# From the scan to the feed-forward: the last chunk computes no state, its row norm moves to the vector engine, and the first gate weights are split in two halves

## The chip, the core and the metric

The kernel runs on one core of a Trainium2 chip. The metric is the device time of one launch in microseconds; lower is better. Engines are named as the profile names them: PE (matrix products and transposes), PEld (its weight loads), DVE, ACT, POOL, and SP, which here only starts transfers.

## The reference

The input `x` has 2048 rows of 512. Each row is normalised, goes through one mixer layer, and then through a mixture of experts:

```python
x = x + attn(layernorm(x))          # attn: the layer below
x = x + experts(layernorm(x))       # 8 experts of width 352, 2 for each row

def attn(x0):
    h = rmsnorm(x0, ln1_w)
    h = x0 + mamba2(h)              # projection, conv, chunked scan, gated norm, out_proj
    h2 = rmsnorm(h, ln2_w)
    return h + silu(h2 @ gate_w) * (h2 @ up_w) @ down_w      # 512 -> 2048 -> 512
# in mamba2, the rows are 16 chunks of 128, with one state per head carried on:
#   states_c = B^T (decay * xdt);  carry_{c+1} = states_c + decay_c * carry_c
#   y_c = Y_diag_c + C_c carry_c ;  out = rmsnorm(y * silu(z), norm_w) @ out_proj_w
```

The state that the last chunk leaves is used by nobody.

## The kernel before, in words

Four stages follow one another, each a block in which every engine has its own list of instructions; all engines meet at the end of a block. `project` makes the products of `in_proj_w` and the convolution; `ssd` is the chunked scan; `feed_forward` is the dense gated layer; `experts` routes the rows and runs the experts. The change lies at the end of `ssd` and the start of `feed_forward`.

**The scan.** The order of the work is written out by hand. A loop runs c = 0 to 17 on every engine. In step c, chunk c is computed (`now`, c < 16), the out projection and row norms of chunk e = c-1 are finished (`late`), and the normed rows of chunk f = c-2 are turned and put into the feed-forward's input (`later`). So step 16 has only e = 15 and f = 14, and step 17 only f = 15. In step 16:

- PE: `out_proj(15, 0)` (12 matmuls L1132), `row_sums(15)` (L1140), `turn_h2(14)` (4 transposes L1154), `out_proj(15, 1)` (12 matmuls). In step 15 it ends with `states(15)` (8 matmuls L1110).
- DVE: `gate(15, 1)`, `low(15, 1)` (L929), `new_carry(15)` (L979), `squares(15)` (L936), `row_sums(15)` (a copy, L941), `h2_low(14)` (L952), `outcome(15)` (L961), which writes the row result `hres`.
- ACT: `high(15, 1)`, `h2_high(14)` (L861), `h_squares(15)` (L874), which sums the squares of `hres`.
- POOL: `row_scale(15)` (L793 to L795), `residual(15)` (L803, `x0 = hres + x0`, which SP then stores as `xh` rows), `second_norm(15)`: two steps on one column (L809, L810), then two on whole rows (L811 `h2 = hres * v`, L812 `h2 = h2 * ln2_row`).

Step 17 is `turn_h2(15)` on PE, `h2_high(15)` on ACT, `h2_low(15)` on DVE. `turn_h2` and `states(15)` contain the same `wait_ge(s["h2_lo"], ...)` several times over.

**The feed-forward.** Its weights come in 8 blocks of 256 of the 2048 columns, and each block has three pieces (gate, up, down; 512 KB each). Each fp32 piece is split into a high and a low part: ACT writes `w_hi` (L1304 for block 0, L1325 later), POOL writes `w_lo = stage - w_hi` (L1278). PE multiplies high by high, high by low and low by high (L1372). A block is run over 4 steps of 512 rows: `width` (two column groups of 128, gate and up, 48 matmuls) and `out` (24 matmuls), with `width` of the next step issued ahead of `out` of this one. ACT takes the silu of a gate product (L1312), DVE multiplies it with the up product (L1338), ACT and DVE split the result (L1315, L1341). In `body(0, 1)` ACT's list has the high part of block 1's gate piece ahead of the silu of step 2:

```python
if k % NR and not (isinstance(b, int) and b == NB - 1):
    j = k % NR - 1
    eng.wait_ge(w_dma[j], b * 16 + 32)
    ...
    eng.activation(w_hi[(k // NR + 1) % 2][j][:, :], stage[j][:, :], ACT.Copy)
following(width, b, k)
```

SP's list in this block: the down piece of block 0 (L1249), the load of all `xh` rows into `acc` (4 MB, L1254), a 10 MB fill of `sorted` with `blank` (L1257), then the pieces of block 1 (L1246, L1249), all on one queue in this order. The gate and up pieces of block 0 are loaded already in step 15 of the scan.

Of the kernel before, what the change touches and what calls it, by code (L numbers as in the profile page):

```python
# [653 lines left out]
def ssd(nc, ins, dr, ident, ones, keep, ffT, first_weights, over):  # L654
# [6 lines left out]
    with ExitStack() as ctx:  # L661
# [94 lines left out]
        def _(eng):  # L756
# [48 lines left out]
            def second_norm(e):  # L805

                t, v = h2[e % 2], small[:, 5:6]
                eng.wait_ge(s["hsq"], e + 1)
                steps = [lambda: eng.tensor_scalar(v, small[:, 4:5], 1.0 / D, EPS, ALU.mult, ALU.add),  # L809
                         lambda: eng.tensor_tensor(v, v, half_neg[:, :], ALU.pow),  # L810
                         lambda: eng.tensor_scalar(t[:, :], hres[:, :], v, None, ALU.mult),  # L811
                         lambda: eng.tensor_tensor(t[:, :], t[:, :], ln2_row[:, :], ALU.mult)]  # L812
                for i, step in enumerate(steps):
                    if i:
                        eng.wait_ge(s["h2_step"], e * NH2 + i)
                    if i == 2:
                        ge(eng, s["h2T"], e - 1)
                    step().then_inc(s["h2_step"], 1)

            eng.wait_ge(s["v_dma"], 16 * 9)  # L820
            for c in range(TILES + 1):
                e = c - 1
                if c < TILES:
                    for a in range(2):
                        skip_x(c, a)
                    decayed_x(c)
                    decay_carry(c)
                if e >= 0:
                    row_scale(e)
                    residual(e)  # L830
                    second_norm(e)

        @block.scalar
        def _(eng):
# [42 lines left out]
            for c in range(TILES + 2):  # L877
                e, f = c - 1, c - 2
                now, late, later = c < TILES, 0 <= e < TILES, 0 <= f
                if now:  # L880
                    exps(c, 0)
                    cum_exp(c, 0)
                    exps(c, 1)
                if late:
                    high(e, 1)
                if now:
                    exps(c, 2)
                if later:
                    h2_high(f)
                if now:  # L890
                    exps(c, 3)
                    cum_exp(c, 1)
                    high(c, 0)
                    if c + 1 < TILES:
                        rows(c + 1)
                if late:
                    h_squares(e)
                if c == 0:
                    eng.wait_ge(s["v_dma"], 16 * 9)
                    eng.wait_ge(s["wo_dma"], 16 * 4)  # L900
                    for n in range(NB):
                        eng.activation(wo_hi[:, n, :], wo_raw[:, n, :], ACT.Copy, scale=normw[:, n:n + 1])\
                           .then_inc(s["wo_hi"], 1)

        @block.vector
        def _(eng):
# [48 lines left out]
            def outcome(e):  # L955
# [5 lines left out]
                eng.scalar_tensor_tensor(hres[:, :], o_ps[:, :], small[:, 3:4], yres[:, :], ALU.mult, ALU.add)\  # L961
                   .then_inc(s["h"], 1)

            def scaled_x(c):
                g, u = group(c)
                eng.wait_ge(s["xb_row"], c + 1)
                ge(eng, s["yd"], 2 * (c - 1))
                ge(eng, s["xdd"], c - 1)
                eng.tensor_tensor(xdt[c % 2][:, :].rearrange("p (g r d) -> p g r d", g=NG, r=HPG),
                                  xb_row[c % 2][:, 0, :].rearrange("p (g d) -> p g d", g=NG).unsqueeze(2)  # L970
                                  .broadcast_to([P, NG, HPG, HD]),
                                  dt_all[:, g, u * HEADS:(u + 1) * HEADS].rearrange("p (g r) -> p g r", g=NG).unsqueeze(3)
                                  .broadcast_to([P, NG, HPG, HD]), ALU.mult).then_inc(s["xdt"], 1)
# [16 lines left out]
            for c in range(TILES + 2):  # L990
# [7 lines left out]
                    score(c, 1)  # L998
                if late:
                    low(e, 1)  # L1000
                    new_carry(e)
                    squares(e)
                if now:
                    gate(c, 0)
                if late:
                    row_sums(e)
                if later:
                    h2_low(f)
                if now:
                    score(c, 2)  # L1010
# [2 lines left out]
                    low(c, 0)  # L1013
                if late:
                    outcome(e)
                if now:
                    if c + 1 < TILES:
                        scaled_x(c + 1)
                    rows_normed(c)
# [7 lines left out]
        def _(eng):  # L1027
# [61 lines left out]
            def states(c):  # L1089

                eng.wait_ge(s["xdd"], c + 1)
                eng.wait_ge(s["xb_row"], min(c + 2, TILES))
                if c == TILES - 1:
                    eng.wait_ge(s["h2_lo"], c - 1)
                if c == TILES - 1:
                    eng.wait_ge(s["h2_lo"], c - 1)
                if c == TILES - 1:
                    eng.wait_ge(s["h2_lo"], c - 1)
                if c == TILES - 1:
                    eng.wait_ge(s["h2_lo"], c - 1)  # L1100
                if c == TILES - 1:
                    eng.wait_ge(s["h2_lo"], c - 1)
                if c == TILES - 1:
                    eng.wait_ge(s["h2_lo"], c - 1)
                if c == TILES - 1:
                    eng.wait_ge(s["h2_lo"], c - 1)
                n = HPG * HD
                for hg in range(NG):
                    a, b = hg // 2, hg % 2
# [10 lines left out]
                    last = eng.transpose(b_ps[:, n * P:(n + 1) * P], cv[c % 2][:, n, :], ident[:, :])  # L1120
                last.then_inc(s["turn"], 1)

            def out_proj(e, a):

                if e == 0 and a == 0:
                    eng.wait_ge(s["wo_lo"], NB)
                if a == 0:
                    ge(eng, s["h"], e)
                eng.wait_ge(s["lo"], 2 * e + a + 1)
                for j in range(HPG):  # L1130
                    for t, (x, w) in enumerate(((y_hi, wo_hi), (y_hi, wo_lo), (y_lo, wo_hi))):
                        mm = eng.matmul(o_ps[:, :], x[a][:, j, :], w[:, a * HPG + j, :],  # L1132
                                        start=(a == 0 and j == 0 and t == 0), stop=(a == 1 and j == HPG - 1 and t == 2))
                mm.then_inc(s["out"], 1)
# [7 lines left out]
            def turn_h2(f):  # L1142

                eng.wait_ge(s["h2_step"], f * NH2 + NH2)
                ge(eng, s["carry"], min(f + 2, TILES))
                ge(eng, s["h2_lo"], f)
                ge(eng, s["h2_lo"], f)
                ge(eng, s["h2_lo"], f)
                ge(eng, s["h2_lo"], f)
                ge(eng, s["h2_lo"], f)  # L1150
                ge(eng, s["h2_lo"], f)
                ge(eng, s["h2_lo"], f)
                for k in range(KD):
                    last = eng.transpose(b_ps[:, k * P:(k + 1) * P], h2[f % 2][:, k * P:(k + 1) * P], ident[:, :])  # L1154
# [3 lines left out]
            for c in range(TILES + 2):  # L1158
# [9 lines left out]
                if now:  # L1168
                    diagonal(c, 0)
                    seg(c, 2)  # L1170
                    carried(c, 0)
                if late:
                    row_sums(e)
                if later:
                    turn_h2(f)
                if now:
                    b_dot_c(c, 1)
                    seg(c, 3)
                    cum_rows(c, 1)
                if late:  # L1180
                    out_proj(e, 1)
                if now:
                    if c + 1 < TILES:
                        rows(c + 1)
                    diagonal(c, 1)
                    carried(c, 1)
                    states(c)


def constants(nc, ident, ones):  # L1190
# [11 lines left out]
def feed_forward(nc, ins, dr, ffT, acc, mv, first_weights, over):  # L1202
# [7 lines left out]
    with ExitStack() as ctx:  # L1210
        def sb(name, shape, dt=F32):
# [14 lines left out]
        assert NI * D == KD * FB and TPR == 4  # L1226
        s = {n: ctx.enter_context(nc.semaphore("ff_" + n)) for n in (
            "blanked", "cleared", "acc_dma", "w_hi", "w_lo",
            "gate_ps", "up_ps", "silu", "prod", "p_hi", "p_lo", "down", "add",
            "bn", "stat")}  # L1230
        CR = 2 * TPR
        w_dma = [over["w_dma0"], over["w_dma1"], over["w_dma2"]]
        block = ctx.enter_context(nc.Block())

        def as_in(t):
            return t[:, :].rearrange("p (k n) -> p k n", k=KD)
# [5 lines left out]
        def _(eng):  # L1242
# [6 lines left out]
                    eng.dma_start(as_down(stage[j]), src).then_inc(w_dma[j], 16)  # L1249

            load_piece(0, 2)
            for i in range(3):
                eng.wait_ge(over[f"xh_st{i}"], 16 * len(range(i, TILES, 3)))
            eng.dma_start(acc[:, :, :], dr["xh"].rearrange("(t p) n -> p t n", p=P)).then_inc(s["acc_dma"], 16)  # L1254
# [12 lines left out]
        def _(eng):  # L1267
# [5 lines left out]

            def low_parts(b, par):
                for j in range(3):
                    eng.wait_ge(w_dma[j], (b + 1) * 16)
                    eng.wait_ge(s["w_hi"], b * 3 + j + 1)
                    eng.tensor_tensor(w_lo[par][j][:, :], stage[j][:, :], w_hi[par][j][:, :].bitcast(F32),  # L1278
                                      ALU.subtract).then_inc(s["w_lo"], 1)

            with eng.Fori(0, NB // 2) as i:
                for par in range(2):
                    low_parts(i * 2 + par, par)

# [16 lines left out]
        def _(eng):  # L1301
            for r in range(3):
                eng.wait_ge(w_dma[r], 16)
                eng.activation(w_hi[0][r][:, :], stage[r][:, :], ACT.Copy).then_inc(s["w_hi"], 1)  # L1304

            def width(b, k):
                step = b * NR + k % NR
# [24 lines left out]
        def _(eng):  # L1332
            def width(b, k):
                for c in range(NI):
# [6 lines left out]
                    eng.tensor_tensor(p_lo[k % 2][:, c, :], prod[c][:, :], p_hi[k % 2][:, c, :].bitcast(F32),  # L1341
                                      ALU.subtract).then_inc(s["p_lo"], 1)

            width(0, 0)
            eng.wait_ge(s["acc_dma"], 16)

# [21 lines left out]
        def _(eng):  # L1368
# [6 lines left out]
            def width(b, k):  # L1375
                par, r = k // NR % 2, k % NR
                cols = slice(r * RG, (r + 1) * RG)
                for c in range(NI):
                    n = (b * NR + r) * NI + c
                    for j, ps, free, done in ((0, gate_ps[c], "silu", "gate_ps"), (1, up_ps[c], "prod", "up_ps")):  # L1380
                        eng.wait_ge(s[free], n + 1)
                        if r == 0 and c == 0:
                            eng.wait_ge(s["w_lo"], b * 3 + j + 1)
                        for q in range(KD):
                            w = [as_in(t[par][j])[:, q, c * P:(c + 1) * P] for t in (w_hi, w_lo)]
                            x = [t[:, q, cols] for t in (hT_hi, hT_lo)]
                            mm = three(ps[:, :], w, x, q == 0, q == KD - 1)
# [537 lines left out]
```

## Time and profile before

| | us |
|---|---|
| median of 3 runs (lowest, highest) | 1609.52 (1608.76, 1609.54) |
| the profiled execution, its whole time | 1608.9 |
| its span, first to last instruction | 1607.2 |
| PE busy over the span | 1432.8 (89%) |
| DVE, ACT, POOL busy over the span | 776.9, 446.9, 441.4 |

The span is the time between the first and the last recorded instruction; 1.7 us of the execution lie around it. Times inside the trace count from the span's start. The scan ends and the feed-forward begins at 598.7 us.

### The profile page before, as it was taken

What the parts mean: (1) busy time and instruction counts of PE and PEld (TensorE: products, weight loads), DVE (VectorE), ACT (ScalarE), POOL (GpSimd) and SP (SyncE); (2) the same over time, 40 slices, a digit from 0 to 9 for tenths busy, and PEclk for the clock granted to TensorE, in tenths of its full rate; (3) what the DMA queues carried; (4) which work ended last, traced back from release to release, by engine and by line L of the source; (5) the groups of instructions that cost most, each with busy time, mean ns of one, the idle gap of its engine ahead of it and who ended that gap; (6) DMA issues with size and microseconds to landing.
All of it is one profiled execution on the core that took longest, in us unless ns stands there. A gap on an engine that the chain in (4) does not pass through costs nothing. (4 is left out here: it accounts for less than half of the span.)

```text
span 1607.2 us, 20104 instructions
## 1 busy us (share of the span) xinstructions
PE 1432.8 (89%) x6651; PEld 1035.5 (64%) x6652; DVE 776.9 (48%) x1357; ACT 446.9 (28%) x924; POOL 441.4 (27%) x486
## 2 busy tenths in 40 slices
PE   5799999799999969999999999999720899999996
PEld 4677778466666648888888888888410555555553
DVE  5868778699999852433333333334544122121211
ACT  3444444545555531222111221111210111111110
POOL 1412111277777661110101101010116122222222
PEclk9899999899999989999999999999865899999998
DMA  8123125432233229100100001000595222222220
GB/s 185 53 78 120 66 79 164 158 130 95 99 113 111 93 63 369 67 27 14 39 13 26 26 13 39 0 1 0 190 369 188 73 74 89 81 87 90 80 86 15
DMA packets 92867, 147.12 MB, mean 92 GB/s; under 512 B 29182, under 2 KB 45566, under 8 KB 92800
## 3 DMA queue, kind: packets, MB, share of 16 engines
q1 hardware_dynamic: 79424, 119.92, 22.7%
q0 software_dynamic: 8800, 25.21, 4.6%
q10 hardware_dynamic: 4576, 1.13, 0.3%
q8 instruction: 37, 0.61, 0.2%
q14 instruction: 30, 0.25, 0.1%
HBM read 91.63 MB, written 58.27 MB: 93 GB/s over the span
## 5 line engine op out<-in xcount | busy, mean ns | idle before, releaser
L1372 PE MATMUL ff_bank<-ff_hT_hi,ff_w_hi 128*128 128x512 f32 x512 | 202.2, 395 | 5.3 <-POOL ff_w_lo L1278 5.3
L1372 PE MATMUL ff_bank<-ff_hT_hi,ff_w_lo 128*128 128x512 f32 x512 | 204.4, 399 | 0.0
L1372 PE MATMUL ff_bank<-ff_hT_lo,ff_w_hi 128*128 128x512 f32 x512 | 202.6, 396 | 0.0
L1814 PE MATMUL ex_bank<-w_gu,xT 128*128 x624 | 192.8, 462 | 1.4 <-ACT xT L1745 0.8
L1338 DVE TENSOR_TENSOR ff_prod<-ff_prod,ff_bank 128x512 f32<-128x512 f32 x64 | 44.1, 688 | 267.2 <-PE ff_bank L1372 253.3
L1278 POOL TENSOR_TENSOR ff_w_lo<-ff_stage,ff_w_hi 128x1024 fp32r<-128x1024 f32 x24 | 57.5, 2400 | 408.2 <-ACT ff_w_hi L1325 408.1
L1814 PEld LDWEIGHTS ex_bank<-w_gu,xT 128*128 128x128 f32 x624 | 116.3, 191 | 60.6 <-issue 3.3
L1784 DVE SCALAR_TENSOR_TENSOR result_rows<-ex_bank,xs,result_rows 128x512 f32<-128x512 f32 x39 | 29.3, 751 | 255.9 <-DMA result_rows<-out_dram,xs 253.3
L599 PE MATMUL pj_bank<-hT_hi,w_in_hi 128*128 128x512 f32 x336 | 137.4, 409 | 10.6 <-DVE zst L525 4.6
L507 DVE SCALAR_TENSOR_TENSOR conv_acc<-raw,conv_w,conv_acc 128x512 f32<-128x512 f32 x144 | 113.9, 791 | 47.0 <-ACT raw L326 37.0
L599 PE MATMUL pj_bank<-hT_lo,w_in_hi 128*128 128x512 f32 x336 | 135.7, 404 | 0.0
L599 PE MATMUL pj_bank<-hT_hi,w_in_lo 128*128 128x512 f32 x336 | 134.3, 400 | 0.0
L1832 PE MATMUL ex_bank<-w_dn,moe_hT 128*128 (+1 forms) x234 | 111.5, 613 | 17.5 <-DVE moe_hT L1779 17.5
L1372 PEld LDWEIGHTS ff_bank<-ff_hT_hi,ff_w_hi 128*128 128x128 f32 x512 | 96.6, 189 | 28.6 <-issue 5.7
L1372 PEld LDWEIGHTS ff_bank<-ff_hT_lo,ff_w_hi 128*128 128x128 f32 x512 | 96.5, 188 | 24.5
L1372 PEld LDWEIGHTS ff_bank<-ff_hT_hi,ff_w_lo 128*128 128x128 f32 x512 | 96.6, 189 | 22.7
L1352 DVE TENSOR_TENSOR acc_rows<-ff_bank,acc_rows 128x512 f32<-128x512 f32 x128 | 87.4, 690 | 40.4 <-PE ff_bank L1372 40.3
L842 ACT ACTIVATE decay<-ss_bank,keep_neg_cum 128x128 f32<-128x128 f32 x256 | 73.3, 370 | 102.5 <-PE ss_bank L1036 102.5
L1372 PE MATMUL ff_bank<-ff_w_lo,ff_p_hi 128*128 128x512 f32 x256 | 100.2, 391 | 0.0
L1372 PE MATMUL ff_bank<-ff_w_hi,ff_p_hi 128*128 128x512 f32 x256 | 100.1, 391 | 0.0
L1312 ACT ACTIVATE ff_prod<-ff_bank 128x512 f32<-128x512 f32 x64 | 38.3, 598 | 221.6 <-PE ff_bank L1372 221.6
L1372 PE MATMUL ff_bank<-ff_w_hi,ff_p_lo 128*128 128x512 f32 x256 | 99.5, 389 | 0.0
(238 smaller groups left out, 2414.6 us busy)
## 6 DMA issues: line engine op xcount, KB each, us to landing
cv_rows<-cst SPq DMA_DIRECT2D x12, 1024.0 KB, 4.2
cv<-cv_rows SPq DMA_DIRECT2D x16, 768.0 KB, 4.3
sorted_rows<-blank SPq DMA_DIRECT2D x1, 10023.0 KB, 43.7
xs<-sorted_rows SPq DMA_DIRECT2D x39, 257.0 KB, 2.7
zs_rows<-zst SPq DMA_DIRECT2D x8, 1024.0 KB, 6.3
zs<-zs_rows SPq DMA_DIRECT2D x16, 512.0 KB, 5.3
w_gu<-in_L_ffn_Wg_dram SPq DMA_DIRECT2D x8, 704.0 KB, 10.7
w_gu<-in_L_ffn_Wu_dram SPq DMA_DIRECT2D x8, 704.0 KB, 11.6
```

The costliest lines, as they stand in the source:

```text
L507: eng.scalar_tensor_tensor(acc[m % 4][:, :], raw[m % 3][:, t:t + GR], conv_w[:, ch, t:t + 1], acc[m % 4][:, :], ALU.mult, ALU.add).then_in ...
L599: mm = eng.matmul(ps[:, :], (w_hi, w_lo)[a][:, k, col:col + P], x[b][:, k, :], start=(k == 0 and t == 0), stop=(k == KD - 1 and t == 2))
L842: last = eng.activation(decay[hg][:, j, :], seg_ps[hg % 2][:, j * P:(j + 1) * P], ACT.Exp, bias=neg_cum[:, g, h:h + 1])
L1278: eng.tensor_tensor(w_lo[par][j][:, :], stage[j][:, :], w_hi[par][j][:, :].bitcast(F32), ALU.subtract).then_inc(s["w_lo"], 1)
L1312: eng.activation(prod[c][:, :], gate_ps[c][:, :], ACT.Silu).then_inc(s["silu"], 1)
L1338: eng.tensor_tensor(prod[c][:, :], prod[c][:, :], up_ps[c][:, :], ALU.mult).then_inc(s["prod"], 1)
L1352: eng.tensor_tensor(row, down_ps[t][:, :], row, ALU.add).then_inc(s["add"], 1)
L1372: mm = eng.matmul(ps, w[a], x[b], start=first and i == 0, stop=last and i == 2)
L1784: eng.scalar_tensor_tensor(rows[:, :], y_ps[v % 2][:, :], xs[v][:, D:D + 1], rows[:, :], ALU.mult, ALU.add).then_inc(s["sum"], 1)
L1814: mm = eng.matmul(ps[:, 0:EI], xT[v % 2][:, k, :], w_gu[:, i, bass.ds(e * KD + k, 1), :].rearrange("p a n -> p (a n)"), start=(k == 0), st ...
L1832: mm = eng.matmul(y_ps[v % 2][:, :], hT[v % 2][0:n, c, :], w_dn[0:n, bass.ds(e * NI + c, 1), :].rearrange("p a n -> p (a n)"), start=(c == ...
```

## The change

In the scan: chunk 15 computes no state (`states`, `decayed_x`, `decay_carry` and `new_carry` are left out for it). In step 16 PE runs `row_sums(15)` between the two halves of `out_proj(15, 1)` and `turn_h2(14)` behind it; DVE runs `h2_low(14)` behind `outcome(15)`. The two whole-row steps of the norm of chunk 15 become one DVE instruction, `last_norm`, and POOL adds the residual behind its two column steps. The repeated waits are taken out (7 in `states`, 6 of 7 in `turn_h2`; the diff shows one of each). In the feed-forward: the first half of block 0's gate piece is split by ACT and DVE, the second half by ACT and POOL; PE waits for the first half, and for the second at the third of its four groups of rows. SP waits for the first half before it loads `acc`.

```diff
@@ ssd, gpsimd @@
-                for i, step in enumerate(steps):
+                for i, step in enumerate(steps[0:2] if e == TILES - 1 else steps):
...
-                    decayed_x(c)
-                    decay_carry(c)
+                    if c + 1 < TILES:
+                        decayed_x(c)
+                        decay_carry(c)
                 if e >= 0:
                     row_scale(e)
-                    residual(e)
+                    if c < TILES:
+                        residual(e)
                     second_norm(e)
+                    if c == TILES:
+                        residual(e)
@@ ssd, scalar @@
                 if later:
                     h2_high(f)
+                if c == TILES:
+                    h_squares(e)
...
-                if late:
+                if late and now:
                     h_squares(e)
@@ ssd, vector @@
+            def last_norm(e):
+                eng.wait_ge(s["h2_step"], e * NH2 + 2)
+                ge(eng, s["h2T"], e - 1)
+                eng.scalar_tensor_tensor(h2[e % 2][:, :], hres[:, :], small[:, 5:6], ln2_row[:, :], ALU.mult, ALU.mult)\
+                   .then_inc(s["h2_step"], 2)
...
                     low(e, 1)
-                    new_carry(e)
+                    if now:
+                        new_carry(e)
                     squares(e)
...
-                if later:
+                if later and c != TILES:
                     h2_low(f)
...
                     outcome(e)
+                if c == TILES:
+                    h2_low(f)
+                    last_norm(e)
@@ ssd, tensor @@
-                if c == TILES - 1:
-                    eng.wait_ge(s["h2_lo"], c - 1)
...
-            def out_proj(e, a):
+            def out_proj(e, a, between=None):
...
                 for j in range(HPG):
+                    if between and j == HPG // 2:
+                        between(e)
...
-                ge(eng, s["carry"], min(f + 2, TILES))
-                ge(eng, s["h2_lo"], f)
+                ge(eng, s["carry"], min(f + 2, TILES - 1))
...
-                if late:
+                if late and now:
                     row_sums(e)
-                if later:
+                if later and c != TILES:
                     turn_h2(f)
...
-                    out_proj(e, 1)
+                    out_proj(e, 1, None if now else row_sums)
+                if c == TILES:
+                    turn_h2(f)
...
-                    states(c)
+                    if c + 1 < TILES:
+                        states(c)
@@ feed_forward, sync @@
             load_piece(0, 2)
+            eng.wait_ge(s["first_lo"], 1)
@@ feed_forward, gpsimd: low_parts @@
+                    cols = slice(KD * FB // 2 if isinstance(b, int) and b + j == 0 else 0, KD * FB)
...
-            with eng.Fori(0, NB // 2) as i:
+            low_parts(0, 0)
+            low_parts(1, 1)
+            with eng.Fori(1, NB // 2) as i:
@@ feed_forward, scalar @@
+                if r == 0:
+                    eng.activation(w_hi[0][0][:, 0:HALF], stage[0][:, 0:HALF], ACT.Copy).then_inc(s["first_hi"], 1)
+                    cols = slice(HALF, KD * FB)
+                eng.activation(w_hi[0][r][:, cols], stage[r][:, cols], ACT.Copy).then_inc(s["w_hi"], 1)
@@ feed_forward, vector, ahead of width(0, 0) @@
+            eng.wait_ge(w_dma[0], 16)
+            eng.wait_ge(s["first_hi"], 1)
+            eng.tensor_tensor(w_lo[0][0][:, 0:HALF], stage[0][:, 0:HALF], w_hi[0][0][:, 0:HALF].bitcast(F32), ALU.subtract)\
+               .then_inc(s["first_lo"], 1)
@@ feed_forward, tensor: width @@
+                            if first:
+                                eng.wait_ge(s["first_lo"], 1)
+                            else:
+                                eng.wait_ge(s["w_lo"], b * 3 + j + 1)
                         for q in range(KD):
+                            if first and r == 0 and c == 0 and q == KD // 2:
+                                eng.wait_ge(s["w_lo"], 1)
```

## Rows read from the trace of the kernel before

**Rows 1.** The page's costliest group: busy us, mean ns, idle before and releaser.

```profile
L1372 PE MATMUL ff_bank<-ff_hT_hi,ff_w_hi 128*128 128x512 f32 x512 | 202.2, 395 | 5.3 <-POOL ff_w_lo L1278 5.3
```

**Rows 2.** Windows: length, busy (x) of PE, PEld, DVE, ACT, POOL; PEclk, DMA share, GB/s.

```profile
592.00:593.00 1.00, 0.00 (x0) 0.00 (x0) 0.00 (x0) 0.00 (x0) 0.81 (x3) 0.53 0.23 88
602.30:605.50 3.20, 3.20 (x8) 2.52 (x9) 0.00 (x0) 2.34 (x2) 3.20 (x2) 0.50 1.00 377
605.50:606.00 0.50, 0.50 (x3) 0.45 (x2) 0.00 (x0) 0.00 (x0) 0.50 (x1) 0.79 1.05 410
606.00:667.00 61.00, 61.00 (x264) 49.36 (x263) 18.91 (x28) 12.60 (x19) 8.06 (x4) 1.00 0.76 260
```

**Rows 3.** Timeline, end of the out projection: start, length, engine, line, operation.

```profile
580.27 1.08 PE L1110 MATMUL ss_bank<-xdd,xb_row 128*64 128x256 f32 x8
...
583.36 0.68 DVE L979 TENSOR_TENSOR carry<-carry,ss_bank 128x512 f32<-128x512 f32 x1
...
583.96 1.89 DVE L936 TENSOR_REDUCE sqs<-sq 128x128 f32<-128x1024 f32 x1
...
585.90 0.38 PE L1140 MATMUL ss_bank<-ones,sqs 128*128 128x2 f32 x2 [1.56 <-DVE sqs L936]
...
586.33 0.63 PE L1154 MATMUL ss_bank<-ident,h 128*128 128x128 f32 x4
...
586.71 0.48 PE L1132 MATMUL ss_bank<-wo_hi,y_hi 128*128 128x512 f32 x1
...
587.00 0.60 ACT L861 ACTIVATE ff_hT_hi<-ss_bank 128x512 fp32r<-128x512 f32 x1 [3.75 <-PE ss_bank L1154]
...
589.79 0.75 DVE L961 SCALAR_TENSOR_TENSOR hres<-ss_bank,small,yres 128x512 f32<-128x512 f32 x1 [1.47 <-PE ss_bank L1132]
```

**Rows 4.** Timeline, from the last row result to the first feed-forward matmul.

```profile
590.57 0.63 ACT L874 ACTIVATE ss_junk<-hres 128x512 bf16<-128x512 f32 x1 [2.98 <-DVE hres L961]
590.62 1.26 POOL L803 TENSOR_TENSOR x<-hres,x 128x512 f32<-128x512 f32 x1 [2.88 <-DVE hres L961]
591.11 0.19 ACT L874 ACTIVATION_READ_ACCUMULATOR ss_junk<-hres 128x1 f32 x1
...
591.97 0.19 POOL L809 TENSOR_SCALAR small<-small 128x1 f32<-128x1 f32 x1
...
592.92 1.59 POOL L811 TENSOR_SCALAR h<-hres,small 128x512 f32<-128x512 f32 x1
...
595.91 1.11 PE L1154 MATMUL ss_bank<-ident,h 128*128 128x128 f32 x4 [6.16 <-POOL h L812]
...
598.67 2.00 ACT L1304 ACTIVATE ff_w_hi<-ff_stage 128x1024 fp32r<-128x1024 f32 x2 [1.02 <-PEq L661]
...
599.82 4.68 POOL L1278 TENSOR_TENSOR ff_w_lo<-ff_stage,ff_w_hi 128x1024 fp32r<-128x1024 f32 x2
...
602.30 0.76 PE L1372 MATMUL ff_bank<-ff_hT_hi,ff_w_hi 128*128 128x512 f32 x1 [5.28 <-POOL ff_w_lo L1278]
```

**Rows 5.** Timeline, two-input operations of DVE and POOL that overlap.

```profile
566.64 1.30 POOL L812 TENSOR_TENSOR h<-h,ln_row 128x512 f32<-128x512 f32 x1
...
566.91 1.58 DVE L946 TENSOR_TENSOR cexp<-cv,ebx 128x512 f32<-128x512 f32 x1
...
579.17 1.27 POOL L803 TENSOR_TENSOR x<-hres,x 128x512 f32<-128x512 f32 x1 [3.59 <-DVE hres L961]
```

**Rows 6.** Durations of single DVE lines: ns min/median/max, first and last start.

```profile
L946 DVE TENSOR_TENSOR cexp<-cv,ebx x32: 684/810/1583, 301.0 to 577.1; 128x512 f32<-128x512 f32 x32
...
L984 DVE TENSOR_SCALAR yres<-x,keep_mean,keep_q x16: 534/536/1531, 314.7 to 579.2; 128x512 f32<-128x512 f32 x16
...
L507 DVE SCALAR_TENSOR_TENSOR conv_acc<-raw,conv_w,conv_acc x144: 720/752/1810, 33.3 to 289.4; 128x512 f32<-128x512 f32 x144
```

**Rows 7.** Timeline, SP's transfers and ACT, at the feed-forward's start and 45 us on.

```profile
599.14 0.40 SPq L1254 DMA_DIRECT2D acc_rows<-xh_rows  x1
...
644.93 1.06 ACT L1325 ACTIVATE ff_w_hi<-ff_stage 128x1024 fp32r<-128x1024 f32 x1 [17.05 <-DMA ff_stage<-in_L_attn_gate_w_dram]
645.90 0.58 ACT L1312 ACTIVATE ff_prod<-ff_bank 128x512 f32<-128x512 f32 x1
...
648.49 0.40 PE L1372 MATMUL ff_bank<-ff_hT_hi,ff_w_hi 128*128 128x512 f32 x1
```

More of the change, by code:

```diff
@@ L1092, in states @@
                 eng.wait_ge(s["xb_row"], min(c + 2, TILES))
-                if c == TILES - 1:
-                    eng.wait_ge(s["h2_lo"], c - 1)
[L1095 to L1106, printed above, removed]
                 n = HPG * HD
@@ L1144, in turn_h2 @@
                 eng.wait_ge(s["h2_step"], f * NH2 + NH2)
-                ge(eng, s["carry"], min(f + 2, TILES))
-                ge(eng, s["h2_lo"], f)
[L1147 to L1151, printed above, removed]
+                ge(eng, s["carry"], min(f + 2, TILES - 1))
                 ge(eng, s["h2_lo"], f)
@@ L1228, in feed_forward @@
             "blanked", "cleared", "acc_dma", "w_hi", "w_lo",
-            "gate_ps", "up_ps", "silu", "prod", "p_hi", "p_lo", "down", "add",
+            "first_hi", "first_lo", "gate_ps", "up_ps", "silu", "prod", "p_hi", "p_lo", "down", "add",
             "bn", "stat")}
@@ L1233, in feed_forward @@
         block = ctx.enter_context(nc.Block())
+        HALF = KD * FB // 2
         def as_in(t):
@@ L1275, in low_parts @@
                 for j in range(3):
+                    cols = slice(KD * FB // 2 if isinstance(b, int) and b + j == 0 else 0, KD * FB)
                     eng.wait_ge(w_dma[j], (b + 1) * 16)
                     eng.wait_ge(s["w_hi"], b * 3 + j + 1)
-                    eng.tensor_tensor(w_lo[par][j][:, :], stage[j][:, :], w_hi[par][j][:, :].bitcast(F32),
+                    eng.tensor_tensor(w_lo[par][j][:, cols], stage[j][:, cols], w_hi[par][j][:, cols].bitcast(F32),
                                       ALU.subtract).then_inc(s["w_lo"], 1)
-            with eng.Fori(0, NB // 2) as i:
+            low_parts(0, 0)
+            low_parts(1, 1)
+            with eng.Fori(1, NB // 2) as i:
                 for par in range(2):
@@ L1303, in _ @@
                 eng.wait_ge(w_dma[r], 16)
-                eng.activation(w_hi[0][r][:, :], stage[r][:, :], ACT.Copy).then_inc(s["w_hi"], 1)
+                cols = slice(0, KD * FB)
+                if r == 0:
+                    eng.activation(w_hi[0][0][:, 0:HALF], stage[0][:, 0:HALF], ACT.Copy).then_inc(s["first_hi"], 1)
+                    cols = slice(HALF, KD * FB)
+                eng.activation(w_hi[0][r][:, cols], stage[r][:, cols], ACT.Copy).then_inc(s["w_hi"], 1)
             def width(b, k):
@@ L1381, in width @@
                         eng.wait_ge(s[free], n + 1)
+                        first = isinstance(b, int) and b + j == 0
                         if r == 0 and c == 0:
-                            eng.wait_ge(s["w_lo"], b * 3 + j + 1)
+                            if first:
+                                eng.wait_ge(s["first_lo"], 1)
+                            else:
+                                eng.wait_ge(s["w_lo"], b * 3 + j + 1)
                         for q in range(KD):
+                            if first and r == 0 and c == 0 and q == KD // 2:
+                                eng.wait_ge(s["w_lo"], 1)
                             w = [as_in(t[par][j])[:, q, c * P:(c + 1) * P] for t in (w_hi, w_lo)]
```

## The prediction, made before the changed kernel was run

> **What bounds the kernel now.** I read the page first, then windows around the passage, then the timeline from 560 to 660 us engine by engine, and last SP's transfers. The page's first group says how much is at stake: ahead of 512 feed-forward matmuls PE sat idle 5.3 us in all, and for one releaser, the low part of the first gate weights on POOL [rows 1]. From there on PE is never idle in the windows (61.00 of 61.00 us between 606 and 667) [rows 2], so the feed-forward's end follows its first matmul, and what comes later follows that end. A microsecond gained before 602.30 is one at the end, unless something in the feed-forward is bound to another clock than PE's. I look for that below, and find one candidate.
>
> The passage itself is one chain with one engine at work at a time. The reader should follow it in [rows 3] and [rows 4]: squares on DVE, row sums and twelve matmuls on PE, `hres` on DVE at 589.79, its squares on ACT, four POOL steps to 595.85, transposes on PE, two evacuations, the block's end at 598.67, ACT's high part, POOL's low part, first matmul at 602.30.
>
> **The change, part by part.**
>
> *Nothing on the path.* `states(15)` takes 1.08 us of PE [rows 3], but it sits ahead of `out_proj(15, 0)`, and the half behind that one waits for `low(15, 1)`, done at 583.4, just before `new_carry` starts. POOL's two state operations of chunk 15 end long before it is needed. The repeated waits: PE's row sums end at 586.28 and the transposes behind seven equal waits start at 586.33 [rows 3], 0.05 us later. I price them at nothing; 0.05 us in each of 15 steps would be 0.7 us, an upper bound.
>
> *The out product.* Without `new_carry`, `squares` starts at 583.36 instead of 583.96: 0.60 earlier. It ends at 583.36 + 1.89 = 585.25, and the row sums start 0.05 later, 585.30. Six of the twelve matmuls are done by then: PE is free from 583.5, and six take 1.4. From the start of the first matmul to `hres` is 589.79 - 586.71 = 3.08 for twelve; the spacing is (3.08 - 0.48) / 11 = 0.236, so six take 3.08 - 1.42 = 1.66. The row sums hold PE for 0.43 (585.90 to 586.33). So `hres` starts at 585.30 + 0.43 + 1.66 = 587.39, and ends at 588.14: 2.40 gained. The row scale on POOL would be ready near 587.1 and does not hold it.
>
> *Squares of hres.* ACT now has `h2_high(14)` ahead of it, and that waits for transposes that PE runs behind the out product, about 587.2 to 587.9. With its 0.60 [rows 3] ACT is free at 588.5, not at 588.17. Then 0.73 (590.57 to 591.30) [rows 4]: 589.25. Gain 2.05, so 0.35 goes back.
>
> *The norm.* Before, POOL was at the residual until 591.88 and took the sum at 591.97, 0.67 after it was there. Now it takes it at about 589.32. The two column steps with their handover are 592.92 - 591.97 = 0.95: 590.27. In place of 1.59 + 1.26 and gaps (592.92 to 595.85 = 2.93) stands one DVE instruction with two SBUF inputs and a column; the nearest line is L507, 0.72 at best, 1.81 at most [rows 6]. I see why it can be more than double: POOL adds the residual in the same moment. POOL need not wait for its own last step and starts a hair ahead of DVE. Where that happened before, with POOL 0.27 ahead, DVE's L946 took 1.58 against 0.684 and ended 0.55 after POOL's operation [rows 5, 6]; with L803 itself only 0.02 ahead, L984 took 1.53 against 0.534 [rows 5, 6]. So from 590.2: 1.27 for the residual and 0.6 behind it, 592.05. Lower bound, if DVE is first: 590.27 + 0.75 = 591.02. I take 592.05, because POOL was first even at 0.02 us. Before it was 595.85, so 3.8 gained (bound 4.85).
>
> The Trainium skill (SBUF — State Buffer, Who interferes with whom) speaks against this edit: a DVE instruction with two SBUF inputs and a POOL operation that reads SBUF exclude each other, and the second to start blocks fully. By that rule the norm would end 1.27 + 0.75 = 2.02 after 590.2, at 592.2, 0.15 later than by the rows.
>
> *Transposes to the block's end* stay at 598.67 - 595.85 = 2.82: block end at 594.87. PE's clock fell between 592 and 593 at 2.7 us after its last matmul [rows 2, 3]; now PE pauses from 587.8 to 592.05, so I leave the transposes and the first matmuls at the lower level, as they were (0.50 until 605.50) [rows 2].
>
> *The halves.* Before, 602.30 - 598.67 = 3.63 from the block's end. Now ACT's half is a 128x512 operation, 0.60 as L861 [rows 3]; DVE's half is one as well, 0.68 as L946 [rows 6]; with three handovers of 0.05 that is 1.45. Gain 2.18. POOL's second half runs about from +1.3 to +2.6, and is needed behind six slow matmuls, at 1.45 + 2.7 = +4.1. POOL's up piece (2.35) ends at +5.0 and is needed behind twelve, eight slow ones in 3.2 and four fast [rows 2], at +5.6 or later. Both are covered. `blank`'s memset on POOL may hold DVE up to 0.3.
>
> PE's first matmul so moves by 3.8 + 2.18 = 6.0, to 596.3.
>
> *What is late next: the queue.* ACT's list has block 1's gate piece ahead of the silu of step 2, and that piece lies on SP's queue behind 14 MB. It came at 644.93 after 17 us of idle ACT; the silu ended at 646.48; PE used the bank at 648.49 [rows 7]. The margin is 2.0 us. PE moves by 6.0, the block's end by 3.8; and the `acc` load, before 0.47 after the block's end [rows 7], now waits for DVE's half and goes out at about +1.5, 1.0 later. If the whole stream starts with it, the gate piece moves by 2.8, and PE stalls for 6.0 - 2.8 - 2.0 = 1.2. If the down piece ahead of it kept the queue busy in that time, the stream moves by 3.8 and PE stalls 0.2. The rows don't say which of the two held `acc`'s packets before, so I take a value between, 0.6.
>
> **Sum.** 2.40 (out product) - 0.35 (ACT order) + 0.60 and 1.15 (POOL takes the sum at once; the row steps) + 2.18 (halves) = 6.0, less 0.6 of new stall: 5.4. Against the profiled execution: 1608.9 - 5.4 = 1603.5. The median of the three runs is 0.6 above it, so 1604.1 for the median.
>
> **The rivals.**
> 1. *DVE gets its norm in first.* Against it: POOL's step to the residual has no wait. It gives 1.05 more, with the transfers moving along: 1603.0. Chance 0.13.
> 2. *No stall at the queue:* 0.6 more, 1603.5. Chance 0.12.
> 3. *PE's clock does not fall.* The pause is 4.3 us where 2.7 was enough before. Transposes 0.5 shorter, and the faster first matmuls then meet the same transfer: 1603.6. Chance 0.05.
> 4. *Most of it is lost to the queue.* The gate piece's landing decides, not PE: the net gain is its shift plus 2.0. If the stream took 45 us plus 2 us or more in its new place, beside the down piece or from waiting on the last `xh` store (out at 591.5), the gain is under 3.2: about 1607. For it: ACT idle 17 us on exactly this; against it: `acc` meets a free queue. Chance 0.13.
> 5. *Slower.* The same mechanism by which it would lose: `acc` waits behind ACT's and DVE's halves. The net is zero when it goes out at 599.14 + 2.0 = 601.1; slower by over 0.2% needs 604.3 or more, 8 us behind my 596.3. Only a hold of the first half behind POOL's whole start (memset, then 4.7 us of low parts) comes near: with 5 us of it, 601.3, 1609.7; with 8, 1612.8. Chance 0.04.
> 6. *The edit does what it says in the scan, but not the halves:* DVE's half waits until POOL's first half-piece is through, 1.3 more: 1605.4. It counts with my forecast's own spread.
>
> **How the numbers follow.** My own case, with 6, has 0.53; its own range is 1603.2 to 1605.8. 0.2% is 3.2 us, about what a measurement here tells from no change; faster means below 1606.3. Cases 1, 2, 3 and my own are all faster: 0.83. Case 4: 0.13, case 5: 0.04. For eight in ten I go from 1602.2 (cases 1 and 2 together, 1602.4) to 1606.8 (into case 4).
>
> **What would show it.** The first L1372 matmul near 596.3 from the span's start, `hres` starting near 587.4, ACT's L874 at 588.5. The norm on DVE about 1.8 long beside L803, not 0.75. `acc` issued near 596.4, and the gate piece of block 1 split by ACT near 641.5. PE idle once by 0.2 to 1.2 us near 642, waiting for ACT's silu. The forecast is wrong if the norm takes 0.75, if that idle is above 2 us, or if the time from PE's first feed-forward matmul to the end of the span changes by more than the stall.

## The result and the profile after

| | before | changed |
|---|---|---|
| median of 5 runs, us | 1609.52 | 1602.09 |
| lowest to highest | 1608.60 to 1609.87 | 1597.25 to 1602.53 |
| profiled execution: time, span | 1608.9, 1607.2 | 1602.53, 1600.8 |

The ratio is 0.9949, 95% interval 0.9932 to 0.9965: faster by 0.5%, 7.4 us where 5.4 was forecast, and 0.1 us outside the stated range (1602.2 to 1606.8). The five runs of the changed kernel lie in two groups, near 1597.4 and 1602.2 (see *The spread*), so the 0.1 by itself says little; the trace says more. The page's group for the first feed-forward product answers to [rows 1]; its releaser is now DVE's half:

```profile
L1388 PE MATMUL ff_bank<-ff_hT_hi,ff_w_hi 128*128 128x512 f32 x512 | 202.5, 396 | 4.4 <-DVE ff_w_lo L1358 3.2
```

The passage in the timeline of the changed kernel (start, length, engine, line, operation), against [rows 3, 4, 7]; step 3 is the fourth and last step of 512 rows of block 0:

```profile
575.92 0.75 DVE L967 SCALAR_TENSOR_TENSOR hres<-ss_bank,small,yres 128x512 f32<-128x512 f32 x1
...
584.91 0.75 DVE L967 SCALAR_TENSOR_TENSOR hres<-ss_bank,small,yres 128x512 f32<-128x512 f32 x1 [1.35 <-PE ss_bank L1137]
...
586.35 0.19 ACT L878 ACTIVATION_READ_ACCUMULATOR ss_junk<-hres 128x1 f32 x1
...
587.43 1.26 POOL L803 TENSOR_TENSOR x<-hres,x 128x512 f32<-128x512 f32 x1
587.55 1.69 DVE L974 SCALAR_TENSOR_TENSOR h<-hres,small,ln_row 128x512 f32<-128x512 f32 x1 [0.90 <-POOL small L810]
...
589.29 1.11 PE L1153 MATMUL ss_bank<-ident,h 128*128 128x128 f32 x4 [4.00 <-DVE h L974]
...
592.04 0.37 SPq L1253 DMA_DIRECT2D ff_stage<-in_L_attn_down_w_dram  x1
593.51 0.37 SPq L1259 DMA_DIRECT2D acc_rows<-xh_rows  x1
593.63 0.77 PE L1388 MATMUL ff_bank<-ff_hT_hi,ff_w_hi 128*128 128x512 f32 x1 [3.22 <-DVE ff_w_lo L1358]
...
640.53 1.06 ACT L1337 ACTIVATE ff_w_hi<-ff_stage 128x1024 fp32r<-128x1024 f32 x1 [20.35 <-DMA ff_stage<-in_L_attn_gate_w_dram]
...
642.13 0.50 PE L1388 MATMUL ff_bank<-ff_hT_hi,ff_w_hi 128*128 128x512 f32 x1 [1.16 <-ACT ff_prod L1324]
```

The reader should see three things. The last but one row result (chunk 14) comes at 575.92, in a part of the scan that the passage does not touch; before it came here:

```profile
578.34 0.75 DVE L961 SCALAR_TENSOR_TENSOR hres<-ss_bank,small,yres 128x512 f32<-128x512 f32 x1
```

So 2.42 us are gained before the passage begins (2.6 since the first row result, which came 0.2 later here). The passage gains 6.25 more up to the first matmul (593.63 against 602.30, less 2.42). And from there to step 3 of block 0 (642.13 against 648.49) 2.31 us go back, of which the profile names 1.16 as PE's idle time for ACT's silu, which waited for the queue. What is left of both, 6.36, is what the span shows (6.4).

### The profile page after: what moved, and what is told of

Same layout as the page of the kernel before. It is cut to its first block and busy times, and to the rows that moved or that the text cites. A ratio compares the mean times of both kernels' runs of the same rounds, so it can differ in the third digit from the quotient of the medians.

```text
span 1600.8 us, 20032 instructions
## 1 busy us (share of the span) xinstructions
PE 1430.9 (89%) x6643; PEld 1034.1 (65%) x6644; DVE 778.4 (49%) x1358; ACT 446.0 (28%) x925; POOL 433.6 (27%) x482
## 3 DMA queue, kind: packets, MB, share of 16 engines
q10 hardware_dynamic: 4576, 1.13, 0.3%
## 5 line engine op out<-in xcount | busy, mean ns | idle before, releaser
L1388 PE MATMUL ff_bank<-ff_hT_hi,ff_w_hi 128*128 128x512 f32 x512 | 202.5, 396 | 4.4 <-DVE ff_w_lo L1358 3.2
L1388 PE MATMUL ff_bank<-ff_hT_hi,ff_w_lo 128*128 128x512 f32 x512 | 204.9, 400 | 0.0
L1388 PE MATMUL ff_bank<-ff_hT_lo,ff_w_hi 128*128 128x512 f32 x512 | 203.1, 397 | 0.0
L1284 POOL TENSOR_TENSOR ff_w_lo<-ff_stage,ff_w_hi 128x1024 fp32r<-128x1024 f32 (+1 forms) x24 | 56.4, 2353 | 409.6 <-ACT ff_w_hi L1337 409.0
L507 DVE SCALAR_TENSOR_TENSOR conv_acc<-raw,conv_w,conv_acc 128x512 f32<-128x512 f32 x144 | 113.9, 791 | 47.5 <-ACT raw L326 37.5
L1388 PEld LDWEIGHTS ff_bank<-ff_hT_hi,ff_w_hi 128*128 128x128 f32 x512 | 96.9, 189 | 28.4 <-issue 3.6
L1388 PEld LDWEIGHTS ff_bank<-ff_hT_lo,ff_w_hi 128*128 128x128 f32 x512 | 96.8, 189 | 24.4
L1388 PEld LDWEIGHTS ff_bank<-ff_hT_hi,ff_w_lo 128*128 128x128 f32 x512 | 96.7, 189 | 22.7
L1388 PE MATMUL ff_bank<-ff_w_lo,ff_p_hi 128*128 128x512 f32 x256 | 100.2, 391 | 0.0
L1388 PE MATMUL ff_bank<-ff_w_hi,ff_p_hi 128*128 128x512 f32 x256 | 100.1, 391 | 0.0
L1388 PE MATMUL ff_bank<-ff_w_hi,ff_p_lo 128*128 128x512 f32 x256 | 99.6, 389 | 0.0
```

The costliest lines, as they stand in the source:

```text
L507: eng.scalar_tensor_tensor(acc[m % 4][:, :], raw[m % 3][:, t:t + GR], conv_w[:, ch, t:t + 1], acc[m % 4][:, :], ALU.mult, ALU.add).then_in ...
L1284: eng.tensor_tensor(w_lo[par][j][:, cols], stage[j][:, cols], w_hi[par][j][:, cols].bitcast(F32), ALU.subtract).then_inc(s["w_lo"], 1)
L1388: mm = eng.matmul(ps, w[a], x[b], start=first and i == 0, stop=last and i == 2)
```

## Experiments

For each kernel I read marks from its one trace, in us, since they separate what the total mixes: the period of a chunk (from row result to row result), and the stretches from the last row result (15) to the block's end, on to the first feed-forward matmul (L1372 before, L1388 changed), and on to the start of the last add of the feed-forward. In brackets stands PE's idle time ahead of step 3. The last column but one is the sum of the three stretches. The stretch from row result 14 to 15 isn't in it: 11.45 before, 8.96 to 9.00 with the changed scan.

| kernel | chunk period | row result to block end | to first matmul | to last add (idle ahead of step 3) | sum | ratio to before, 95% interval |
|---|---|---|---|---|---|---|
| before | 17.51 | 8.87 | 3.64 | 535.9 (0) | 548.4 | 1 |
| changed | 17.31 | 7.13 | 1.59 | 538.4 (1.16) | 547.1 | 0.9949, 0.9932 to 0.9965 |
| changed, again | 17.32 | 7.15 | 1.59 | 537.4 (0.21) | 546.2 | 0.9949, 0.9935 to 0.9962 |
| one wait | 17.32 | 8.87 | 3.64 | 537.2 (0) | 549.7 | 0.9974, 0.9963 to 0.9984 |
| more waits | 17.82 | 8.86 | 3.64 | 536.3 (0) | 548.8 | 1.0029, 1.0017 to 1.0041 |
| POOL waits | 17.32 | 8.86 | 3.64 | 535.9 (0) | 548.4 | 0.9983, 0.9973 to 0.9992 |
| waits back | 17.50 | 6.68 | 1.59 | 537.6 (1.19) | 545.9 | 0.9955, 0.9942 to 0.9969 |
| no halves | 17.31 | 7.14 | 3.64 | 536.0 (0) | 546.7 | 0.9957, 0.9940 to 0.9974 |
| acc early | 17.32 | 7.15 | 1.58 | 537.0 (0) | 545.7 | 0.9947, 0.9928 to 0.9965 |
| pieces first | 17.32 | 7.14 | 1.59 | 536.9 (0) | 545.6 | 0.9955, 0.9940 to 0.9970 |
| residual last | 17.32 | 5.75 | 1.59 | 537.4 (1.13) | 544.7 | 0.9953, 0.9938 to 0.9969 |
| three edits | 17.32 | 5.72 | 1.59 | 537.4 (1.19) | 544.7 | 0.9937, 0.9923 to 0.9951 |
| residual and pieces | 17.31 | 5.75 | 1.59 | 536.1 (0) | 543.4 | 0.9936, 0.9923 to 0.9950 |

**The repeated waits.** *One wait:* the kernel before, with this alone:

```diff
@@ turn_h2 (and the same in states) @@
-                ge(eng, s["h2_lo"], f)
-                ge(eng, s["h2_lo"], f)
-                ge(eng, s["h2_lo"], f)
-                ge(eng, s["h2_lo"], f)
-                ge(eng, s["h2_lo"], f)
-                ge(eng, s["h2_lo"], f)
```

> The kernel before, with one of each group of repeated waits kept in turn_h2 and states and nothing else changed. Theory W (each repeated wait on PE costs about 0.03 us, six in a chunk 0.19): the chunk period falls from 17.51 to 17.32 us from chunk 3 on, the last row result comes 2.4 to 2.6 us earlier, and the time is 1606.9 to 1607.2, 0.16% faster. Rival (what moved the scan in the changed kernel is another edit or chance, and the waits are free, as the prediction had it): period 17.51, time 1609.5.

*More waits:* the kernel before with six of these lines added.

> The kernel before with thirteen instead of seven equal waits in turn_h2. Theory W: six more cost another 0.19 us for each chunk from the fourth on, period 17.70, time 1612.1. Rival (waits are free, or only an overlap that the seventh wait has used up): period 17.51, time 1609.5.

The period went to 17.32, as expected, and to 17.82, where 17.70 was expected. On the same chip the kernel before had a median of 1607.77, the one with one wait 1603.72, the one with thirteen 1612.96. These are moves of 4.1 and 5.2 us where the periods up to chunk 14 explain 2.6 and 4.1; in the profile of thirteen waits 1.95 more went in the last chunk (13.40 instead of 11.45), where the last nine matmuls of the out projection ran at the lower clock. The rest is within the intervals. The place shows in the spacing of the row sums and the transposes behind the waits in one chunk. Before, with seven waits:

```profile
537.39 0.38 PE L1140 MATMUL ss_bank<-ones,sqs 128*128 128x2 f32 x2
537.85 0.63 PE L1154 MATMUL ss_bank<-ident,h 128*128 128x128 f32 x4
```

With one:

```profile
534.20 0.38 PE L1128 MATMUL ss_bank<-ones,sqs 128*128 128x2 f32 x2
534.44 0.63 PE L1136 MATMUL ss_bank<-ident,h 128*128 128x128 f32 x4
```

With thirteen:

```profile
540.64 0.38 PE L1140 MATMUL ss_bank<-ones,sqs 128*128 128x2 f32 x2
541.41 0.63 PE L1160 MATMUL ss_bank<-ident,h 128*128 128x128 f32 x4 [0.39 <-issue]
```

From start to start 0.24, 0.46 and 0.77 us: the first six waits behind the one cost 0.22, the next six 0.31. The second figure is 0.05 us for a wait that is long satisfied. That the first is smaller because the matmul in front still covers some of them is my reading; no run shows it.

*POOL waits:* the kernel with one wait, and six more of these in POOL's `row_scale`:

```diff
                 eng.wait_ge(s["rsum"], e + 1)
+                eng.wait_ge(s["rsum"], e + 1)
```

> The kernel before without the repeated waits on PE, but with six repeated waits in POOL's row_scale of each chunk, where POOL had slack. Theory W (a repeated wait costs the engine that runs it, and the time only where that engine sets the chunk's period): period 17.32 as without them. Rival (repeated waits cost wherever they stand, or by their bulk in the program): period 17.5 or more.

The period stayed 17.32. On POOL, with slack, such waits cost nothing; on PE, which sets the period, they do, and it isn't the bulk of the program.

*Waits back:* the changed kernel with the seven lines in `turn_h2`.

> The changed kernel with the seven equal waits of turn_h2 put back, nothing else. If the prediction's sum was right but for the waits: chunk period 17.51, the passage and the stall as in the changed kernel, the time 2.4 to 2.6 us above the changed kernel on the same chip and 4.8 to 5.4 us below the kernel before, ratio near 0.9968. If the passage itself gave more than forecast: ratio at 0.995.

The period came back to 17.50, and the median was 2.1 us above the changed kernel run beside it (1601.72 against 1599.66). The ratio, 0.9955, lies between the two expectations (0.9968 and 0.995), and its interval holds both: the ratio can't decide, the trace has to. This execution's first row result came at 331.3 and not at 333.3 as before (see *The spread*). From the row result of chunk 14 to the last add it took 554.9 (1131.0 - 576.12) against 559.9 before (1138.2 - 578.34): 5.0, near the 5.4 that was forecast for the passage. Of these 5.0 some came from the clock: the four transposes ran at the full clock here (0.66 instead of 1.11), after the same pause of 4.00 us as in the changed kernel, and the block's end came 6.68 after the row result instead of 7.13.

**The queue.** *No halves:* the changed scan with the feed-forward stage of before.

> The changed kernel with the feed-forward stage as it was before: no halves, no wait of SP before the acc load; the scan as changed. Theory Q (the landing of block 1's gate piece on SP's queue sets PE's fourth step, so that what the halves give PE is lost again): first L1372 matmul about 3.6 us after the block's end instead of 1.6, no idle or under 0.3 us ahead of step 3, and the time equal to the changed kernel's within 0.5 us, 1601.7 to 1602.3. Rival (halves worth their 2.0 us less a stall of 1.3): 0.7 to 1 us slower than the changed kernel, 1602.9 or more.

*Acc early:* the changed kernel with SP's wait moved.

```diff
             load_piece(0, 2)
-            eng.wait_ge(s["first_lo"], 1)
...
             eng.dma_start(acc[:, :, :], dr["xh"].rearrange("(t p) n -> p t n", p=P)).then_inc(s["acc_dma"], 16)
+            eng.wait_ge(s["first_lo"], 1)
             eng.wait_ge(s["blanked"], 2)
```

> The changed kernel with SP's wait for the first half moved from ahead of the acc load to behind it (ahead of the 10 MB fill). Theory Q: acc goes out 0.5 us after the block's end instead of 1.5, the gate piece of block 1 lands 0.5 to 1.0 us earlier relative to the block's end, PE's stall ahead of step 3 falls from 1.3 to 0.3 to 0.8 us, and the time falls by as much, to about 1601.3. Rival (the queue is held by the down piece and the fill, not by when acc is issued): landing and stall as in the changed kernel, 1602.1.

*Pieces first:* the changed kernel with the loads of block 1's gate and up pieces between the acc load and the fill.

```diff
+            for j in range(2):
+                eng.wait_ge(s["w_lo"], j + 1)
+                load_piece(1, j)
             eng.wait_ge(s["blanked"], 2)
...
-            with eng.Fori(1, NB) as b:
+            eng.wait_ge(s["w_lo"], 3)
+            load_piece(1, 2)
+            with eng.Fori(2, NB) as b:
```

> The changed kernel, with the gate and up pieces of block 1 put on SP's queue ahead of the 10 MB fill, behind the acc load. Theory Q: ACT's 20 us wait for the gate piece goes, PE has no idle ahead of step 3 whatever acc does, and from the row result to the last add of the feed-forward it takes 1.3 us less than in the changed kernel (545.8 instead of 547.1). Rival (the stall has another cause in ACT's list): the idle of 1.2 to 1.5 us ahead of step 3 stays.

Without the halves the first matmul comes 2.05 later and the last add comes no later: 546.7 against 547.1 and 546.2. As changed, the halves bought nothing that the traces show. With acc early the acc load went out 0.5 after the block's end, and the gate piece was there 45.8 us behind it, 46.3 after the block's end; in the changed kernel it was 47.0 and 48.5, in its second trace 46.1 and 47.5. So it came 1.2 to 2.2 earlier, where 0.5 to 1.0 was expected:

```profile
589.41 0.37 SPq L1253 DMA_DIRECT2D ff_stage<-in_L_attn_down_w_dram  x1
589.89 0.40 SPq L1258 DMA_DIRECT2D acc_rows<-xh_rows  x1
...
635.74 1.06 ACT L1337 ACTIVATE ff_w_hi<-ff_stage 128x1024 fp32r<-128x1024 f32 x1 [18.13 <-PE ff_bank L1388]
```

(The profile puts this wait down to PE, but the gate piece, issued at 595.75, took 39.9 to land, up to 635.65: it was the transfer.) PE's idle was gone here and with the pieces first, and the sum fell to 545.7 and 545.6, by 0.5 to 1.5 against the two traces of the changed kernel. The rival on each (another limit of the queue, another cause in ACT's list) is out by the traces. The times can't tell these kernels apart: the ratios 0.9947, 0.9949, 0.9955 and 0.9957 have intervals that overlap almost wholly.

**The norm.** *Residual last:* the changed kernel with

```diff
                     if c == TILES:
+                        eng.wait_ge(s["h2_step"], e * NH2 + NH2)
                         residual(e)
```

> The changed kernel, with POOL made to wait for DVE's norm of chunk 15 before it adds the residual. Theory P (POOL's residual keeps DVE's norm waiting): the norm takes 0.75 us instead of 1.69, and it ends 0.85 to 0.94 us earlier after the row result; the block's end follows by as much. Since everything behind the block's end moves with it, the queue too, the time falls by 0.9 us, if the clock returns at the same point. Rival (a scalar_tensor_tensor of three SBUF operands takes 1.7 us by itself): 1.69 stays, nothing moves.

```profile
587.43 0.75 DVE L975 SCALAR_TENSOR_TENSOR h<-hres,small,ln_row 128x512 f32<-128x512 f32 x1 [0.90 <-POOL small L810]
...
588.24 0.66 PE L1154 MATMUL ss_bank<-ident,h 128*128 128x128 f32 x4 [3.06 <-DVE h L975]
588.26 1.26 POOL L803 TENSOR_TENSOR x<-hres,x 128x512 f32<-128x512 f32 x1 [0.92 <-DVE h L975]
```

The norm takes 0.75. The block's end came 1.38 earlier after the row result, 0.45 more than expected: the transposes still ran at the full clock (0.66 instead of 1.11). PE's pause ahead of them was shorter, 3.06 instead of 4.00, but that alone doesn't decide it: with the waits back the pause was 4.00 and the clock was full too. And the stall of 1.13 ahead of step 3 stayed.

*Three edits:* residual last, acc early, and `h_squares(15)` ahead of `h2_high(14)` on ACT.

> The changed kernel with the residual behind DVE's norm, SP's wait moved behind the acc load, and ACT's squares of chunk 15 ahead of the evacuation of chunk 14. Expected from the parts: 0.9 us from the residual, 1.3 from the queue, 0.2 to 0.35 from ACT's order: from the row result to the last add 544.6 instead of 547.1, and 2.5 us, 0.15%, less than the changed kernel, if the clock returns at the same point. If the gains hide each other: less than 1.5 us.

The sum is 544.7, as expected (544.6), but not from the expected parts: the residual alone has it too. ACT's order gained 0.1 and DVE's `h2_low(14)` then stood in the norm's way; and the acc load, free of its wait, waited for the store of the last `xh` rows, which now came later in relation to the block's end (issued 590.33 and 2.0 us to land; acc at 592.36, 1.06 after the block's end). The idle of 1.19 was back: on the queue the gains hid each other. The number was met because residual last itself had gained more than was expected of it.

*Residual and pieces:* residual last with pieces first.

> The changed kernel with the residual behind DVE's norm and with the gate and up pieces of block 1 ahead of the 10 MB fill. From the parts: from the row result to the last add of the feed-forward 544.7 less the stall of about 1.4 that was left there, 543.3 with the clock back after 3.5 us, up to 544.5 with it back after 6; no idle ahead of step 3; about 2.6 us, 0.16%, below the changed kernel on the same chip, and the fastest of all. Rival (the two gains hide each other, as in the three edits together): 544.5 or more and the idle comes back.

543.4 and no idle, as expected: 2.7 below the changed kernel run beside it in the trace, and 2.0 in the medians (1597.70 against 1599.66), though the two intervals overlap. By the trace it is the fastest version of the study; by the ratio it is level with the three edits (0.9936 and 0.9937).

**The spread.** *Changed, again:*

> The changed kernel itself once more, on the same chip as the other two, as what they are to be compared with. Its five runs had lain in two groups, near 1597.4 and 1602.2. Expected: ratio 0.9949 to 0.9957 to the kernel before, from the row result to the last add 547.1 less or more 0.6 with the clock's return; if the two groups are the spread of every kernel here, the others show it too.

The ratio came out as 0.9949 again. Its five runs went from 1597.17 to 1602.88, and the kernel before from 1606.16 to 1611.94 in 17 runs on another chip: the width is not the change's. Part of it lies ahead of the change. The windows from 300 to 330 us (length, PE busy, PEclk, DMA share, GB/s) of this kernel and then of acc early, whose code is the same up to there:

```profile
300.00:330.00 30.00, 22.51 (x151) 0.84 0.33 118
```

```profile
300.00:330.00 30.00, 22.66 (x159) 0.94 0.27 101
```

The first row result comes at 333.75 in one and 330.88 in the other. All 13 traces follow this: seven with a clock of 0.84 or 0.85 in this window have it at 333.3 to 334.1, five with 0.93 or 0.94 at 330.9 to 331.7, and one wait, with 0.88, at 332.0. The kernel before and the changed kernel both had 0.85, so the 6.4 us between their profiles don't hold this. Of the 4.7 us between the spans of the two kernels above it is 2.9; 0.4 lie in the sum, and 1.4 behind the last add. Whether the two groups of the changed kernel differ in the same way isn't shown: no trace of it comes from the faster group.

## Why the prediction was wrong

By its own steps, gains counted from the row result of chunk 14. Two steps failed, the first and the last of this list, with opposite signs:

- *Nothing on the path*: the step that put the time outside the range. I priced the repeated waits at nothing, with 0.7 us as the bound, since the transposes start 0.05 after the row sums' end [rows 3]. That end is modelled; what counted was start to start. They cost 0.19 a chunk in 13 chunks, 2.4 us, over three times the bound. The trace of before had it in view: its first period (chunk 0 to 1, with no waits in `turn_h2`) is 17.33, the others 17.5. I had not compared them. With 2.4 us more the median would be 1604.5, inside the range and 0.4 from the forecast.
- *The out product*: forecast 2.40, measured 2.46 (584.91 against 589.79, less 2.42).
- *Squares*: forecast 2.05, measured 2.34. ACT's evacuation was through 0.3 earlier than I had it.
- *The norm*: forecast 3.8, measured 4.2 (589.24 against 595.85, less 2.42). POOL was first by 0.12 us, the residual held DVE for 0.94, and the norm ended 0.55 behind POOL's operation, as L946 had [rows 5]. The Trainium skill's rule (SBUF — State Buffer, Who interferes with whom) would have put it 0.75 behind; the order and the size of the hold agree, the tail is shorter. Rival 1 did not happen, and residual last shows its price: 0.94.
- *The halves*: forecast 1.45 from the block's end, measured 1.59.
- *The first matmul*: forecast 6.0, measured 6.25.
- *What is late next*: the right place and the right mechanism, the wrong size. I took 0.6, between 0.2 and 1.2; 2.31 were lost between the first matmul and step 3. By the prediction's own formula (PE's gain, less the gate piece's, less the margin) that is 6.25 - 1.98 - 2.0 = 2.3: the gate piece came 4.40 earlier (640.53 against 644.93), of which 2.42 are the waits', and so 1.98, and not the 2.8 or more that I had counted on. The block's end gained 4.2 and `acc` went out 1.0 later behind it, as in my upper case, which leaves 3.2; the other 1.2 are the queue's, which took 47.0 us from there where it had taken 45.8 (644.93 - 599.14). That part I had at nothing in my own case; rival 4 had it, as 2 us or more. In the second trace of the changed kernel the queue took 46.1 and the same sum gives 1.3: which of the two an execution gets, and why, stays open.

The profile shows only 1.16 of the 2.31 as idle time, since PE itself was slower up to there. In this window of the changed kernel (length, PE busy, PEclk, DMA share, GB/s) its clock is at the lower level for over 5 us, against 3.2 [rows 2]:

```profile
593.63:599.00 5.37, 5.37 (x13) 0.50 0.80 258
```

That is not an effect of the edit: the feed-forward stage of before, started elsewhere in time, had it for 3.1 (POOL waits), 4.1 (more waits) and 6.1 us (one wait), with 535.9, 536.3 and 537.2 to the last add. Nor did it cost anything here: where the queue binds, slow matmuls only take the place of idle time. Changed again (lower level for over 5 us, idle 0.21) and residual last (3.3 us, idle 1.13), with the same 46.1 on the queue, both needed 537.4 to the last add.

So the passage gave 3.9 where 5.4 was forecast (to the last add 3.8, and by that mark 4.7 in changed again and 5.0 with the waits back), the waits 2.4 where nothing was, and the sum in the profile is 6.4. That this lies within 1.0 of the forecast is luck: an error of 2.4 and one of 1.7 on the queue offset each other. The median's further 1.0 lies within the spread of the runs. Rival 2 (no stall) did not happen. Rival 3 (the clock stays up) did not happen in the changed kernel, but did for the transposes with the waits back and with the residual last. Rivals 4 and 5 named the mechanism that did take part of the gain, in too large a size. One sign of being wrong that the prediction named for itself was met: from the first feed-forward matmul to the end of the span it took 1007.2 instead of 1004.9 us, 2.3 more, where 0.6 of stall was forecast.

## What to carry to other kernels

Price every instruction in the queue of the engine that sets the period, waits that are satisfied too, and check it between iterations of the same trace that have them and have not; a gap to a modelled end shows nothing. When a chain is shortened, look for what starts at the block's boundary and not at the chain's end: here a 14 MB queue decided what PE's earlier start was worth. The split of the first weights was worth nothing (547.1 and 546.2 against 546.7 without it) until the acc load no longer waited for it (545.7). Two gains that meet at the same queue have to be measured together. When a step is moved to DVE, ask what POOL starts at that moment: making POOL wait for the norm gave 0.94 us.

## What was not expected of the hardware

- Satisfied waits on PE cost 0.03 us each behind one (six of them 0.19 us a chunk) and 0.05 us each behind seven (six of them 0.31 us), on POOL with slack nothing.
- One feed-forward stage, in the same code, needed 3.1 to 6.1 us after its first matmul until PEclk rose from 0.50 to 1.00, which went with 1.3 us more to the last add.
- After the same pause of 4.00 us the same four transposes ran at the lower clock in one trace (1.11 us) and at the full clock in another (0.66 us).
- A queue of equal bytes was through 45.4 to 46.0 us behind the acc load with the down piece 0.5 us ahead of it (six traces), and 46.1 to 47.0 us with it 1.5 us ahead (four traces).
